# Storing the split q and k once in DRAM, in an order that three runs of terms can be read from

## What is computed

```python
q = (x @ wq.T).reshape(Bx, Tx, H, Dh).transpose(0, 2, 1, 3)   # k and v alike
attn = jnp.einsum('bhqd,bhkd->bhqk', q, k) / scale
attn = attn + slopes[None, :, None, None] * dist[None, None, :, :]   # dist = -|i - j|
attn = jax.nn.softmax(attn, axis=-1)
out = jnp.einsum('bhqk,bhkd->bhqd', attn, v)
x = layernorm(x + out @ wo.T + bo)
h = silu(w1(x)) * w2(x); h = gelu(h1(h)); h = gelu(h2(h)); x = layernorm(x + w3(h))
```

## Time and profile before

| what | value |
|---|---|
| time, median of 3 runs | 779.03 us (771.1 to 779.26) |
| time of the profiled execution | 778.99 us |
| its span in the profile | 777.0 us |
| PE busy, PE weight loads busy | 744.8 us (96%), 542.4 us (70%) |
| DVE, ACT, POOL busy | 641.2, 598.6, 355.1 us |
| chain that ended last: PE, DVE, issue, DMA, SP | 80%, 5%, 4%, 3%, 3% |
| DMA: moved, mean rate | 88.72 MB, 114 GB/s |
| DMA share of the 16 engines' time: us 40 to 400, us 450 to 777 | 0.68, 0.26 |

### The profile page before, as it was taken

The page is one execution under the profiler, slowest core; times in us unless marked ns, Lnnn a source line. Parts: engine busy times, 40 slices in busy tenths (PEclk is TensorE's granted clock), DMA queues, the critical chain, the costliest instruction groups (busy, mean ns, idle before and its releaser), DMA issues.

```text
span 777.0 us, 26998 instructions
## 1 busy us (share of the span) xinstructions
PE 744.8 (96%) x10262; PEld 542.4 (70%) x10262; DVE 641.2 (83%) x1316; ACT 598.6 (77%) x1083; POOL 355.1 (46%) x528
## 2 busy tenths in 40 slices
PE   5899999999999999999999999999999999999995
PEld 3566756676667676676765788887777777778874
DVE  4799989999899999998994767888777777777875
ACT  5588878788788888887888777777777777777773
POOL 5257969788576766666654301122221122221212
PEclk8699999999999999999999999999999999999998
DMA  5767767776656666666631112223222233332221
GB/s 159 181 175 163 192 161 195 177 189 175 158 156 150 171 172 166 168 149 166 156 102 51 36 33 48 61 54 68 57 57 59 56 68 68 68 68 65 59 54 57
DMA packets 177117, 88.72 MB, mean 114 GB/s; under 512 B 67760, under 2 KB 164080, under 8 KB 177008
## 3 DMA queue, kind: packets, MB, share of 16 engines
...
HBM read 49.39 MB, written 37.22 MB: 111 GB/s over the span
## 4 chain that ended last, share of the span: by engine, by line
PE 80%; DVE 5%; issue 4%; DMA 3%; SPq 3%; ACT 2%; POOL 1%; DVEq 0%; POOLq 0%; ACTq 0%
PE ps_o L583 17%; PE ps_b L1054 13%; PE ps_b L1057 13%; PE ps_a L505 12%; PE ps_b L513 6%; PE ps_b L640 3%; PE ps_b L601 3%; PE ps_a L520 2%; PE ps_a L1054 2%; PE ps_a L1057 2%; PE ps_a L623 2%; PE ps_a L609 2%; PE ps_b L520 2%; DVE gate_f L1274 2%; PE ps_b L631 1%
## 5 line engine op out<-in xcount | busy, mean ns | idle before, releaser
L829 DVE TENSOR_REDUCE neg_sb<-ps_a 128x2 f32<-128x512 f32 x512 | 322.0, 681 | 30.2 <-PE ps_a L520 23.8
L718 ACT ACTIVATE probs<-ps_b 128x512 f32<-128x512 f32 x512 | 275.7, 595 | 52.5 <-PE ps_b L520 36.7
L505 PE MATMUL ps_a<-qk_stack 52*64 52x256 bf16 x2048 | 174.8, 281 | 8.8 <-DMA qk_stack<-qk_scratch 6.6
L513 PE MATMUL ps_b<-qk_stack 54*64 54x256 bf16 x2048 | 168.5, 276 | 4.4 <-issue 2.9
L1168 ACT ACTIVATE gelu_f<-ps_b,sc 128x512 f32<-128x512 f32 x124 | 85.4, 689 | 77.0 <-PE ps_b L1057 76.3
L583 PE MATMUL ps_o<-probs,v_aug 128*32 128x256 f32 x2048 | 139.2, 387 | 2.7 <-issue 2.7
L505 PEld LDWEIGHTS ps_a<-qk_stack 52*64 52x64 bf16 x2048 | 83.7, 108 | 81.2 <-DVE neg_sb L829 40.6
L520 PE MATMUL ps_a<-corner_sb,eye_sb 64*64 64x128 bf16 x1024 | 116.7, 222 | 0.0
L520 PE MATMUL ps_b<-corner_sb,eye_sb 64*64 64x128 bf16 x1024 | 113.9, 218 | 0.0
L1054 PE MATMUL ps_b<-g2h,h_hi 128*128 128x512 f32 x256 | 102.2, 399 | 1.8 <-DVE gate_f L1274 1.6
L1054 PE MATMUL ps_b<-g1h,h_hi 128*128 128x512 f32 x256 | 101.3, 396 | 0.1
...
## 6 DMA issues: line engine op xcount, KB each, us to landing
...
```

The source lines that it names most:

```text
L505: pe.matmul(ps[side * TILE:(side + 1) * TILE, qb * SEQ:(qb + 1) * SEQ], q_stack[i][rows_of, j, at:at + TILE], k_stack[i][rows_of, j, :], s ...
L513: pe.matmul(ps[side * TILE:(side + 1) * TILE, kb * SEQ:(kb + 1) * SEQ], k_stack[i][rows_of, j, at:at + TILE], q_stack[i][rows_of, j, :], s ...
L718: nc.scalar.activation(probs[:, h % HALF, :], ps_b[b_bank(t, k)][:], ACT.Exp, scale=slope[h]).then_inc(exp_done, 1)
L829: nc.vector.tensor_reduce(negmax[:, h_a // HALF, h_a % GROUPS, h_a % HALF // GROUPS, :], ps_a[a_bank(t, k)][:].rearrange("p (b k) -> p b k ...
```

## The change

Batches 1 to 31 are stored differently. Each of the three parts of q and of k is written once, into ten places of the scratch tensor of which six are filled: q0 q1 q2 k2 k1 k0. Counted from place n, pairs of places that stand 3, 4 or 5 apart give the six products: (q0 k2)(q1 k1)(q2 k0), (q0 k1)(q1 k0), (q0 k0). So the spill becomes three DMAs of 128 KB, one as soon as each part is there, 384 KB in all. The stack is read back in three runs of terms and two groups: six DMAs of 192, 192, 128, 128, 64 and 64 KB, for all heads at once, in pieces of 4 KB. Their destinations are 24, 16 and 8 partitions. The order of terms in the stack changes, their sum doesn't. PE waits once for the whole stack. Batch 0 keeps its old terms and pieces in a scratch tensor of its own, so the spill of batch 2 no longer waits for batch 0's stack. Nothing on PE, DVE, ACT or POOL is added, removed or moved.

The diff, without the lines that only pass the new tensor on:

```diff
@@ -70,7 +70,10 @@
 KB = KA + MPARTS
 OCOLS = VCOLS // 2
 SLOTS = BLK * HEADS
-SPILLS = 5
+SPILLS_FIRST = 5
+SPILLS = 3
+RUNS = 3
+PLACES = 10
 SQUARE = 32
 XT_BUFS = 6
 
@@ -312,8 +315,8 @@
         qk_done, qk_copied, qk_first, qk_left = sem("qk_done"), sem("qk_copied"), sem("qk_first"), sem("qk_left")
         qk_second, qk_split = sem("qk_second"), sem("qk_split")
         spilled = sem("spilled")
-        stacked = [[sem(f"stacked{i}_{half}") for half in range(2)] for i in range(2)]
-        pair_landed = [sem(f"pair_landed{j}") for j in range(2)]
+        stacked = [sem(f"stacked{i}") for i in range(2)]
+        first_landed = [sem(f"first_landed{j}") for j in range(4)]
         v_done, v_copied = sem("v_done"), sem("v_copied")
         scores_a, max_done = sem("scores_a"), sem("max_done")
         mT_done, m_copied, m_first, m_split = sem("mT_done"), sem("m_copied"), sem("m_first"), sem("m_split")
@@ -361,10 +364,10 @@
         tail.ps_r = [ps_b[(last_norm + 1 + o) % B_BANKS] for o in range(KT)]
 
 
-        def spill_last(eng, b, par):
-
-            parts, terms = qk_sb[par], qk_dram[par].rearrange("n r d h t -> n (d h) r t")
-            wait(eng, qk_split, b + 1)
+        def spill_last(eng):
+
+            parts, terms = qk_sb[0], qk_first_dram.rearrange("n r d h t -> n (d h) r t")
+            wait(eng, qk_split, 1)
             eng.dma_start(terms[0, :, 0:3, :], parts[:, 0:3, 0, :]).then_inc(spilled, DMA)
             eng.dma_start(terms[:, :, 5, :].rearrange("n p t -> p n t"),
                           parts.rearrange("p r n t -> p (r n) t")[:, 0:6:5, :]).then_inc(spilled, DMA)
@@ -375,30 +378,43 @@
             sp.dma_start(wk_sb[:], wkT).then_inc(qk_const_landed, DMA)
             sp.dma_start(rows_sb, rows).then_inc(rows_landed, DMA)
 
-            def spill(b, par):
-
-                parts, terms = qk_sb[par], qk_dram[par].rearrange("n r d h t -> n (d h) r t")
-                wait(sp, qk_first, b + 1)
+            def spill_first():
+
+                parts, terms = qk_sb[0], qk_first_dram.rearrange("n r d h t -> n (d h) r t")
+                sp.wait_ge(qk_first, 1)
                 sp.dma_start(terms[1, :, 0:3, :],
                              parts[:, 0, 1, :].unsqueeze(1).broadcast_to([P, 3, SEQ])).then_inc(spilled, DMA)
-                wait(sp, qk_second, b + 1)
+                sp.wait_ge(qk_second, 1)
                 sp.dma_start(terms[1, :, 3:5, :],
                              parts[:, 1, 1, :].unsqueeze(1).broadcast_to([P, 2, SEQ])).then_inc(spilled, DMA)
                 sp.dma_start(terms[0, :, 3:5, :], parts[:, 0:2, 0, :]).then_inc(spilled, DMA)
-                if b > 0:
-                    spill_last(sp, b, par)
-
-            def stack_part(b, pairs, signal):
-
-                src = qk_dram[b % 2].rearrange("n r d (g j) t -> g (r d) n j t", g=GROUPS)
+
+            def spill(b, par):
+
+                parts, places = qk_sb[par], qk_dram[par].rearrange("s d h t -> (d h) s t")
+                sp.wait_ge(qk_first, b + 1)
+                sp.dma_start(places[:, 0:6:5, :], parts[:, 0, :, :]).then_inc(spilled, DMA)
+                sp.wait_ge(qk_second, b + 1)
+                sp.dma_start(places[:, 1:5:3, :], parts[:, 1, :, :]).then_inc(spilled, DMA)
+                sp.wait_ge(qk_split, b + 1)
+                sp.dma_start(places[:, 2:4, :], parts[:, 2, :, :]).then_inc(spilled, DMA)
+
+            def stack_first(pairs, signal):
+
+                src = qk_first_dram.rearrange("n r d (g j) t -> g (r d) n j t", g=GROUPS)
                 for g in range(GROUPS):
-                    dst = qk_stack[b % STACKS][g * TILE:g * TILE + STACK, :, pairs, :]
+                    dst = qk_stack[0][g * TILE:g * TILE + STACK, :, pairs, :]
                     sp.dma_start(dst.rearrange("p n j t -> p n (j t)"),
                                  src[g, :, :, pairs, :].rearrange("r n j t -> r n (j t)")).then_inc(signal, DMA)
 
-            def stack(b, half):
-
-                stack_part(b, slice(half * HH, (half + 1) * HH), stacked[b % 2][half])
+            def stack(b, run):
+
+                apart, count, row = ((3, 3, 0), (4, 2, 3 * DH), (5, 1, 5 * DH))[run]
+                src = qk_dram[b % 2][0:2 * apart].rearrange("(n s) d (g j) t -> g n s d (j t)", n=2, g=GROUPS)
+                for g in range(GROUPS):
+                    dst = qk_stack[b % STACKS][g * TILE + row:g * TILE + row + count * DH, :, :, :]
+                    sp.dma_start(dst.rearrange("p n j t -> p n (j t)"),
+                                 src[g, :, 0:count].rearrange("n s d c -> (s d) n c")).then_inc(stacked[b % 2], DMA)
 
             def max_rows(b, i, hf):
 
@@ -411,12 +427,12 @@
             def step(t, s):
                 par = s % 2
                 if live(t + 2, BATCH) and t + 2 > 0:
-                    wait(sp, spilled, (t + 3) * SPILLS * DMA)
+                    sp.wait_ge(spilled, (SPILLS_FIRST + (t + 2) * SPILLS) * DMA)
                     wait(sp, scores_b, (t - 1) * HEADS)
                     if t + 2 < STACKS:
                         sp.wait_ge(rows_laid[t + 2], 2)
-                    for half in range(2):
-                        stack(t + 2, half)
+                    for run in range(RUNS):
+                        stack(t + 2, run)
                 if live(t + 5, BATCH):
                     wait(sp, v_done, t)
                     wait(sp, xT_landed, (t + 5) * DMA)
@@ -432,18 +448,16 @@
                 if live(t + 1, BATCH) and t >= -1:
                     max_rows(t + 1, (s + 1) % STACKS, 0)
                 if live(t + 3, BATCH):
-                    for half in range(2):
-                        wait(sp, stacked[1 - par][half], (t + 3) // 2 * GROUPS * DMA)
-                        if t + 3 == 2:
-                            sp.wait_ge(pair_landed[half], GROUPS * DMA)
-                    spill(t + 3, 1 - par)
+                    if t + 3 == 0:
+                        spill_first()
+                    else:
+                        wait(sp, stacked[1 - par], (t + 2) // 2 * RUNS * GROUPS * DMA)
+                        spill(t + 3, 1 - par)
                 if t == FIRST:
-                    sp.wait_ge(spilled, SPILLS * DMA)
+                    sp.wait_ge(spilled, SPILLS_FIRST * DMA)
                     sp.wait_ge(rows_laid[0], 2)
-                    for j in range(2):
-                        stack_part(0, slice(j, j + 1), pair_landed[j])
-                    stack_part(0, slice(2, HH), stacked[0][0])
-                    stack(0, 1)
+                    for pairs, landed in zip((slice(0, 1), slice(1, 2), slice(2, HH), slice(HH, HG)), first_landed):
+                        stack_first(pairs, landed)
                 if live(t + 1, BATCH):
                     max_rows(t + 1, (s + 1) % STACKS, 1)
 
@@ -526,10 +540,10 @@
                 i_a = (s + (1 if k < HEADS - AHEAD else 2)) % STACKS
                 in_a, in_b = live(b_a, BATCH), live(t, BATCH)
                 if in_a:
-                    if b_a == 0 and h_a in (0, GROUPS):
-                        pe.wait_ge(pair_landed[h_a // GROUPS], GROUPS * DMA)
-                    elif h_a == (2 * GROUPS if b_a == 0 else 0) or h_a == HALF:
-                        wait(pe, stacked[b_a % 2][h_a // HALF], (b_a // 2 + 1) * GROUPS * DMA)
+                    if b_a == 0 and h_a in (0, GROUPS, 2 * GROUPS, HALF):
+                        pe.wait_ge(first_landed[h_a // GROUPS if h_a < HALF else 3], GROUPS * DMA)
+                    elif b_a > 0 and h_a == 0:
+                        pe.wait_ge(stacked[b_a % 2], (b_a + 1) // 2 * RUNS * GROUPS * DMA)
                     to_a = take_a(t, k)
                 if in_b:
                     if k % HALF == 0:
@@ -748,7 +762,7 @@
                         act.wait_ge(rows_landed, DMA)
                         lay_rows(t - FIRST, 1)
                         if t == FIRST:
-                            spill_last(act, 0, 0)
+                            spill_last(act)
                         if t == FIRST + 2:
                             lay_rows(2, 0)
 
@@ -897,7 +911,8 @@
 
                 wait(pool, qk_copied, b + 1)
                 wait(pool, qk_split, b)
-                wait(pool, spilled, (b - 1) * SPILLS * DMA)
+                if b > 1:
+                    pool.wait_ge(spilled, (SPILLS_FIRST + (b - 2) * SPILLS) * DMA)
                 nc.gpsimd.tensor_copy(parts[:, 0, :, :], qk_f[:]).then_inc(qk_first, 1)
                 wait(pool, qk_first, b + 1)
                 nc.gpsimd.tensor_tensor(qk_rest[:], qk_f[:], parts[:, 0, :, :], ALU.subtract).then_inc(qk_left, 1)
@@ -1368,7 +1383,8 @@
 
     x1_dram = nc.dram_tensor("x1_scratch", [BATCH * SEQ, D], F32, kind="Internal").ap()
     y_dram = nc.dram_tensor("y_scratch", [BATCH * SEQ, D], F32, kind="Internal").ap()
-    qk_dram = nc.dram_tensor("qk_scratch", [2, 2, TERMS, DH, HEADS, SEQ], BF16, kind="Internal").ap()
+    qk_first_dram = nc.dram_tensor("qk_first_scratch", [2, TERMS, DH, HEADS, SEQ], BF16, kind="Internal").ap()
```

(1 more changed line is left out.)

4 lines of the change are left out of this document (2 added, 2 removed).

## The result

The changed kernel takes 823.55 us (median of 4 runs, 818.51 to 827.44) where the kernel before takes 776.95 us (4 runs, 771.1 to 779.26). The ratio is 1.0595, with a 95% interval of 1.0539 to 1.0651: some 46 us slower, and outside the range of the forecast. The profiled execution took 827.42 us, its span was 825.4 us.

A forecast was written before the change was run, and what follows sets the result against it. PE, busy 96% of the span, was taken as the bound, with 9.95 us lost around idle times. 778.99 + 0.5 (start) - 1.9 (stores) = 777.6 us, loads 0; range 768.5 to 788 us.

The forecast's parts named there:

- Loads, steady state. Value taken: 0: Stack loads in each step: six issues instead of four delay later loads 0.9 us, hidden by about 9 us; worth 0.
- the 1.76 of the earlier trace: Steady state of the kernel before: 1.76 us lost per us of PE idleness, with the clock lowered after one idle time.
- Rival 1: Stack loads: unequal engines make the burst 1.07 us longer on the engine carrying PE's code; 790.9 us, chance 0.22.
- Stores 0 directly, -1.9 us through the idle times: Steady-state stores: PE never waits for them, but smaller stores ahead of late code fetches shorten four idle times; -1.9 us.
- The idle times are tied to the burst: Steady state: PE runs dry because its code packet isn't served until SP's burst of loads drains, some 5.4 us later.
- Rival 2: Steady state: a light engine carries the code, or wider issue spacing lets it in; all 9.95 us go, 769.5 us, chance 0.30.
- The start, +0.5 us: Batch 1 at the start: earlier store against two more loads and a wait for the whole stack; +0.5, between -0.5 and +1.5.
- What the profile after would show: Signs in the profile: three 128 KB spill rows, six kinds of loads, mean DMA share from 0.68 to about 0.56.
- The 12.17 us step: Steady state: a step still lasts 12.17 us where nothing is idle.
- I have missed a contention: The prediction's stated conclusion should the steady-state step not stay at 12.17 us where nothing is idle.
- Rival 3: Steady state: the bytes are in nothing's way, idle times come by chance of phase; 771 to 780 us, inside the main case.

The follow-up runs named there:

- Experiments 2: The changed kernel with the old six-term stores (768 KB in five DMAs) put back, new loads kept: 826.49 us, 1.0581 of before.
- 6: The changed kernel with each of its six loads cut into two halves of the heads (twelve loads, 2 KB pieces), one wait: 774.7 us, 0.9978 of before.
- 15: The changed kernel with each load cut in two, q and k apart (twelve loads, 4 KB pieces), one wait: 777.69 us, 0.9967 of before.
- 8: The kernel before, with PE waiting at head 0 for both halves of the stack: 780.89 us, 1.0039 of before.
- experiment 1: The kernel before with probe loads put in front, single and in sets: the old four loads take 4.3 us, the changed kernel's six 6.6 us.
- 7: The changed kernel with twelve loads by halves of the heads, first halves issued first, PE waiting for each half: 773.31 us, 0.9971 of before.
- 11: The changed kernel with 512 KB stored, runs of 32 and 16 rows in halves (eight loads), PE waiting for each half: 769.01 us, 0.9888 of before.

## Why the prediction was wrong

*The step that failed is "Loads, steady state. Value taken: 0".* It rested on "the same 9 us cover that PE now waits for all of it at head 0", and "the cover would be gone at a landing more than 4 us later, which no row suggests". Both numbers were off. The 4 us put the landing of a whole stack some 5 us after its first issue, and no row of mine had it. It was 6.54 us, head 0 came after 8.29, so the room in the kernel before was 1.8 us in the median. And the landing moved by 2.9 us, to 9.47. Experiments 2 (stores excluded), 6 and 15 (same rows, no loss) and 8 (single wait excluded) leave the way in which the loads are cut as the cause. In us 40 to 400, scaled to the same work, PE's idle time grew by 31 us, some 25 of them waits for the stack (21.7 x 1.136) and 7 idle times with "issue" (11.2 x 1.136 - 5.8), and the time by 49. That is 1.6 us for each us of idleness, near the 1.76 of the earlier trace rows, and the granted clock fell to 0.50 behind a wait here too. The prediction also left out the weight pieces of steps 2 to 12, in which 27.6 of the 48.4 us were lost.

*Rival 1 had the direction, not the size, and only the smaller victim.* "Slower, the burst lasts longer", by 12, 16 and 8 engines: the counts were borne out (experiment 1). But "1.07 us longer" came from bytes per engine at 15 KB/us, and the set takes 2.3 us longer; and the price was put on PE's code alone, 790.9 us, when PE's wait at head 0 was the larger part. Unequal engines alone aren't the reason either: twelve loads with the same unequal engines lose nothing. Rival 1's own sign, "issue" idle times over 2 us, is there too, as a smaller part (before, PE's rows of this kind sum to 5.8 us in the window; after to 11.2, of which three rows stand here). Waits of after, us 40 to 400:

```profile
PE ps_b L527 <- issue: 4.7, 4, 1.7
PE ps_o L597 <- issue: 3.5, 1, 3.5
PE ps_a L534 <- issue: 1.7, 3, 0.6
```

*"Stores 0 directly, -1.9 us through the idle times."* The 0 held within the noise: 2 and the change differ by less than their intervals. The -1.9 is too small to show in that pair, where the "issue" idle times are 9.4 us with the old stores and 11.2 with the new.

*The idle times are tied to the burst.* This was only taken from order of time, and the traces bear it out. Each of the 14 idle times of PE over 0.3 us with "issue" as releaser (five before, nine after, us 40 to 400) ends 1.3 to 1.6 us after a 16 KB packet of q8 has landed. The longest of after, 3.47 us, and the code queue in us 175.5 to 178.2, with no q8 packet in the 11.7 us ahead:

```profile
178.22 0.45 PE L597 MATMUL ps_o<-probs,v_aug 128*32 128x256 f32 x1 [3.47 <-issue]
```

```profile
q8 instruction: 1, 0.02, 2.6%
```

This packet started at 175.57, and the last piece of a stack landed at 175.81. Before, the packets behind all five idle times started 0.1 to 0.7 us ahead of the last landing of a stack; after, five of nine started within 0.7 us of one, among them those behind the four idle times over 1 us. So for the long ones the reading holds that a code packet isn't served before the burst has drained, though no view names the request. The other four of after, 0.5 to 0.9 us, started up to 5.4 us ahead of it.

What takes these idle times away isn't an early landing. Kernels 6, 7, 11 and 15, with eight or twelve loads a stack, have none or 0.3 us of them, and their stacks land later than before's; what they share is a DMA share of 0.49 to 0.54 and loads that don't pile up. That they alone were worth 8.9 us in kernel 11 (769.01 against 777.88 in the same series) isn't shown either: 6, 7 and 15 lack them too and gain 0.2 to 0.3%. Rival 2's time (769.5) was thus reached by another kernel; its first mechanism, a light engine, plays no part in a kernel whose 16 engines carry the same.

*The start, +0.5 us.* PE's first scores of batch 1 came 3.4 us later. Same step, same error: the landing was costed by its issue alone (+1.4 us), and the slower set (2.3 us) was missing. The loads of batch 1 were issued 1.1 us earlier than before (21.28 against 22.37) and took 8.93 us instead of 6.56.

*What the profile after would show.* Three stores of 128 KB and six kinds of loads: right. DMA share down to 0.56: wrong, 0.65 in place of 0.68, over a stretch with 12% fewer steps; the longer time of the pieces took up what the fewer bytes gave. The 12.17 us step: wrong; the 30 steps between head 0 of batch 1 and of batch 31 last 14.0 us on average, 12.5 before, and "I have missed a contention" applies. Rival 3's 771 to 780 us fell with the result, and its "chance of phase" leaves out what all 14 idle times above have in common.

What stays open: the issue times show that twelve loads of a stack don't pile up and that six do, and a piece takes 219 ns in the one case and 390 in the other (24, 16 and 8 rows). That piling up is what slows the pieces is my reading; no run spaced the same six loads out. Piece size, order of groups and rows per engine were excluded as the only cause, and the mechanism inside the queue wasn't found.
